# Splitting the expert weights in 24 pieces over the block loop instead of one expert an iteration

## The chip, the cores and the metric

One NeuronCore of one Trainium2 chip runs the whole kernel. The metric is the device time of one execution in microseconds. Five engines work side by side and meet only at semaphores: TensorE (PE; its weight loads are shown as PEld), VectorE (DVE), ScalarE (ACT), GpSimd (POOL), and SyncE (SP), which here only issues DMAs. ACT issues DMAs too.

## What is computed

64 images of 224 x 224 are embedded as 197 tokens of 192 features each (12,608 tokens); local attention (12 heads, 6 neighbours to each side) and a mixture of experts (2 of 8) follow, both with a residual:

```python
h = tok(x)                                   # patches @ W + b, class token, + pos_embed
h = h + local_attn(layernorm(h))             # window of +-6 tokens, 12 heads of 16
xn = layernorm(h)
top_w, top_i = top_k(softmax(xn @ router_w.T), 2);  top_w /= top_w.sum()
for e in range(8):
    w_e = sum(top_w * (top_i == e))
    out += w_e * (gelu(xn @ w1[e] + b1[e]) @ w2[e] + b2[e])      # 192 -> 768 -> 192
h = h + out
```

The products run in 16 bits with each 32-bit operand split in two halves: hi = f16(64 w), lo = f16(64 w - hi). For the expert weights the kernel makes those halves itself, from the f32 weights in HBM.

## The kernel before

There are two parts, one after the other. `attention_part` (some 935 us) embeds, attends, routes, and scatters the routed rows to a scratch in HBM, sorted by expert. `experts_part` (the rest) runs 73 batches of 384 sorted rows through the experts, with the split weights `w1s`, `w2s` that the first part leaves in SBUF.

`attention_part` goes over 53 blocks of 240 tokens. Every engine runs its own unrolled loop `pipeline(eng, body)` over iterations t = 0 to 61, and in iteration t each stage of the work has a block of its own: embedding, statistics and first normalisation have block t, the qk and v products t - 1, the scores t - 3, softmax and the product with v t - 4, projection and second normalisation t - 5, the router product t - 6. So from t = 53 on there is nothing to embed. Routing proper (choosing two experts, counting places) runs for two blocks at once: its part 0 on DVE in odd iterations, its parts 1, 2 and 3 in even ones. Between part 1 and part 2 TensorE counts with matmuls over `marks` (L794). Each engine's order within an iteration is that of its `body`:

- TensorE: counts (even t), turn of `xs`, of `os`, of `prob` (L812), of `payload`, qk product (L832), router (L844), v (L851), projection (L863), product with v (L877), scores (L885, L893), and then the 24 f32 matmuls of the next embedding (L775, 4.1 us).
- DVE: second normalisation, routing part 1, sum of the embedding (L644), statistics, part 2, first normalisation (L568), part 3, part 0 (begins at L594), low half of qk (L670), residual `h2` (L683), statistics, `on` (L694), the **expert split** (L700, L702), row maximum (L708), shift (L713).
- ACT: issue of the **expert's load** (L454, L455), issue of four `k_diag` copies (L461), exp (L465), `payload` (L471), `xT` (L481), `oT`, `xT2`, `pT`, `logit` (L505), qk high half (L511), v, `xs` (L522), issue of the `h2` output (L528), the **expert's high halves** (L536, L537), `os` (L542).
- POOL: low halves (L401, L413, L423), the reciprocal roots (L381, L384), and the scatter of the routed rows by indirect DMA (L391), four an iteration.

An expert's weights come as two loads, `stage1` [128, 3, 768] (1152 KB) and `stage2` [128, 6, 192] (576 KB), into one buffer each. `expert_loaded(t)` gives expert t - 1 for t = 1 to 7, and expert 7 for t = 53. In that iteration ACT issues both loads at the top (after DVE is through with the expert before) and multiplies near its end; DVE subtracts before it takes up the scores:

```python
act.wait_ge(s["staged"], 32 * (e + 1))
act.mul(w1s[0][:, e], stage1[:], WS)
act.mul(w2s[0][:, e], stage2[:], WS).then_inc(s["split_hi"], 1)
```

SP waits in iteration 56 until all experts are split, since the tables at the end of the part lie in `stage1`.

Of the kernel before, what the change touches and what calls it, by code (L numbers as in the profile page):

```python
# [21 lines left out]
ALU = mybir.AluOpType  # L22
# [88 lines left out]

EARLY = 7


def expert_loaded(t):


    if 1 <= t <= EARLY:  # L120
        return t - 1
    if BLOCKS <= t < BLOCKS + EXPERTS - EARLY:
        return t - BLOCKS + EARLY
    return None


def vit_tower(nc, xt, w_embed, bias_tab, pos, w_qk, w_v, w_p, b_p, router, w1, b1, w2, b2,
# [19 lines left out]
def attention_part(nc, xt, w_embed, bias_tab, pos, w_qk, w_v, w_p, b_p, router, w1, w2, b1, ident, band,  # L147
# [6 lines left out]
    with ExitStack() as ctx:  # L154
# [124 lines left out]
        def _(sp):  # L279
# [28 lines left out]
            def body(t):  # L308
                g, a = t - 2, t - 4
                if runs(t, 4):  # L310

                    sp.wait_ge(s["qk_lo_set"], min(a + 2, BLOCKS))
                    need(sp, s["scored"], 2 * a)
                    for h in range(8):
                        sp.dma_start(*key_halves(h, a)).then_inc(s["k_diag_set"], 16)
                if runs(t, 3):
                    load_band(t - 3)

                if runs(t, 0) and t > 0:
                    need(sp, s["embedded"], t - 1)  # L320
                    sp.dma_start(patches[t % 2][:], xt[t]).then_inc(s_patch[t % 2], 16)
                    need(sp, s["h1_set"], t - 1)
                    load_tab(t)
                if runs(t, 2):

                    sp.wait_ge(s["v_set"], g + 1)
                    sp.dma_start(v_dram[REACH + SPAN * g:REACH + SPAN * g + SPAN, :].rearrange("(n p) c -> p n c", n=2),
                                 v_rows[:].rearrange("p n h d -> p n (h d)")).then_inc(s["v_out"], 16)
                if runs(t, 4):

                    if a == 0:
                        sp.wait_ge(s["pad_set"], 32)
                    sp.wait_ge(s["v_out"], 16 * min(a + 2, BLOCKS))
                    need(sp, s["pv_done"], a)
                    for r in range(TRIO):
                        src = bass.AP(v_handle, SPAN * a * VCOLS + r * QUADS * (DH + 1),
                                      [[VCOLS, KEYS], [QUERIES * VCOLS, WINDOWS], [1, QUADS * (DH + 1)]])
                        cols = slice(r * QUADS * (DH + 1), (r + 1) * QUADS * (DH + 1))
                        sp.dma_start(v_diag[r * KEYS:(r + 1) * KEYS, :, cols], src).then_inc(s["v_in"], 16)
                if t == EARLY - 1:  # L340
                    sp.dma_start(b1s[:], b1).then_inc(s["later_in"], 16)
                if t == BLOCKS + 2:
                    sp.wait_ge(s["embedded"], BLOCKS)
                    sp.dma_start(fill_rows, fill).then_inc(s["later_in"], 16)
                if t == BLOCKS + 3:
                    sp.wait_ge(s["split_lo"], EXPERTS)
                    sp.dma_start(number, numbers).then_inc(s["later_in"], 16)
                    sp.dma_start(base, region_at[0:1, :]).then_inc(s["later_in"], 16)

# [82 lines left out]
        def _(act):  # L432
# [13 lines left out]

            def body(t):
                f, g, a, c, d, b = t, t - 1, t - 3, t - 4, t - 5, t - 6
                e = expert_loaded(t)
                if e is not None:  # L450
                    if e == 0:
                        act.wait_ge(s["setup2"], 2)
                    need(act, s["split_lo"], e)
                    act.dma_start(stage1[:], w1[e]).then_inc(s["staged"], 16)  # L454
                    act.dma_start(stage2[:], w2[e]).then_inc(s["staged"], 16)  # L455
                if runs(t, 3):
# [66 lines left out]
                if runs(t, 5):  # L523
# [5 lines left out]
                    else:  # L529
                        for n in range(2):  # L530
                            rows = tile_rows(d, n)
                            act.dma_start(out[at + ROWS * n:at + ROWS * n + rows, :], h2[0:rows, n, :]).then_inc(s["h2_out"], 16)
                if e is not None:

                    act.wait_ge(s["staged"], 32 * (e + 1))
                    act.mul(w1s[0][:, e], stage1[:], WS)  # L536
                    act.mul(w2s[0][:, e], stage2[:], WS).then_inc(s["split_hi"], 1)  # L537
                if runs(t, 4):

# [8 lines left out]
        def _(dve):  # L548
# [83 lines left out]
            def body(t):  # L632
# [28 lines left out]
                                             op0=ALU.mult, op1=ALU.subtract).then_inc(s["setup2"], 1)  # L661
                if due:
                    route_steps(grp, 3)
                if due_0:
                    route_steps(grp_0, 0)
                if runs(t, 1):
# [20 lines left out]
                if runs(t, 4):  # L687
# [5 lines left out]
                    need(dve, s["o_lo_set"], c)  # L693
                    dve.tensor_tensor(on[:].rearrange("p n (h e) -> p n h e", h=HEADS), o[:, :, :, 0:DH],  # L694
                                      rden[:].unsqueeze(3).to_broadcast([128, 2, HEADS, DH]), ALU.mult).then_inc(s["norm_done"], 1)
                e = expert_loaded(t)
                if e is not None:

                    dve.wait_ge(s["split_hi"], e + 1)
                    dve.scalar_tensor_tensor(out=w1s[1][:, e], in0=stage1[:, 0:2, :], scalar=WS, in1=w1s[0][:, e, 0:2, :],  # L700
                                             op0=ALU.mult, op1=ALU.subtract)
                    dve.scalar_tensor_tensor(out=w2s[1][:, e], in0=stage2[:], scalar=WS, in1=w2s[0][:, e],  # L702
                                             op0=ALU.mult, op1=ALU.subtract).then_inc(s["split_lo"], 1)
                if runs(t, 3):

                    for n in range(2):
# [481 lines left out]
```

## Time and profile before

| | us |
|---|---|
| median of 3 runs | 1693.18 |
| lowest, highest | 1689.94, 1693.35 |
| the profiled execution | 1697.55 |
| its span | 1695.8 |
| its attention part, about | 935 |

| engine | busy us | share of the span |
|---|---|---|
| TensorE (PE) | 1491.4 | 88% |
| DVE | 1121.2 | 66% |
| POOL | 861.2 | 51% |
| ACT | 718.4 | 42% |

The profile is of one execution. A slice of the page's time lines is 1/40 of the span, 42.4 us; a digit is a share in tenths. In what follows "interval t" is the time from the start of L644 (DVE's sum for block t) to the same instruction for block t + 1: it comes once an iteration and marks the beat of the pipeline.

### The profile page before, as it was taken

The numbers are of one execution on the slowest core, as the hardware profiler recorded it, in microseconds if no ns is written. First come the engines' busy times: TensorE is split into PE (matmuls) and PEld (weight loads), VectorE is DVE, ScalarE is ACT, GpSimd is POOL, SyncE is SP. The second block draws the span as 40 slices with busy tenths as digits, with TensorE's granted clock in tenths as the row PEclk, the third lists the DMA queues.
The fourth block names the chain that finished last, engine by engine and source line by source line (L and its number), as shares of the span: only waits on it lengthen the run. The fifth ranks groups of instructions, "written<-read, shape, count | busy, mean of one in ns | idle before, by whom it ended". The sixth has DMA issues, their size and how long they took to land. (4 is left out here: it accounts for less than half of the span.)

```text
span 1695.8 us, 52298 instructions
## 1 busy us (share of the span) xinstructions
PE 1491.4 (88%) x18345; PEld 1238.1 (73%) x18346; DVE 1121.2 (66%) x2875; ACT 718.4 (42%) x1201; POOL 861.2 (51%) x900
## 2 busy tenths in 40 slices
PE   4777999999999999899562799999999999999995
PEld 4666888888888788788451577777777777777774
DVE  3466777778777776777645466666666666666663
ACT  2443444444444444444421444444444444444441
POOL 3122656656555555555535155545554555455544
PEclk9887999999999999999865799999999999999998
DMA  6654555555555555555422334443444334433432
GB/s 206 205 172 126 157 148 154 153 151 155 144 150 154 150 152 145 143 139 150 113 76 95 93 59 60 60 65 57 59 60 65 57 59 60 65 58 59 59 45 29
DMA packets 190164, 182.64 MB, mean 108 GB/s; under 512 B 86361, under 2 KB 166437, under 8 KB 188989
## 3 DMA queue, kind: packets, MB, share of 16 engines
q1 hardware_dynamic: 125834, 111.46, 23.7%
q0 software_dynamic: 41680, 41.84, 16.8%
q10 hardware_dynamic: 22499, 27.28, 4.9%
q8 instruction: 101, 1.65, 0.4%
q14 instruction: 50, 0.41, 0.1%
HBM read 104.93 MB, written 65.29 MB: 100 GB/s over the span
## 5 line engine op out<-in xcount | busy, mean ns | idle before, releaser
L988 POOL DMA_INDIRECT out<-y,token x219 | 368.5, 1683 | 73.7 <-issue 72.9
L1096 PE MATMUL down<-w_hi,g_hi 128*128 x1314 | 323.7, 246 | 1.9 <-DVE y L1062 1.1
L1098 PE MATMUL down<-w_hi,g_lo 128*128 x1314 | 323.0, 246 | 0.0
L1097 PE MATMUL down<-w_lo,g_hi 128*128 x1314 | 322.9, 246 | 0.0
L1084 PE MATMUL up<-e_xT,w_hi 128*128 128x384 f16 x1314 | 286.7, 327 | 0.0
L1009 ACT ACTIVATE act_out<-up,bias 128x384 f32<-128x384 f32 x438 | 250.9, 581 | 73.3 <-PE up L1084 73.2
L391 POOL DMA_INDIRECT sorted_scratch<-payload,place x212 | 219.5, 1035 | 59.9 <-issue 56.9
L775 PE MATMUL near<-we,patches 128*120 128x192 f32 x1272 | 226.2, 335 | 17.4 <-DMA patches<-in_xt 10.0
L1001 ACT COPY e_xT<-turned 128x1152 f16<-128x1152 f16 x73 | 81.6, 1118 | 353.8 <-PE turned L1076 353.8
L775 PEld LDWEIGHTS near<-we,patches 128*120 128x120 f32 x1272 | 210.2, 187 | 27.8 <-issue 27.7
L1045 DVE TENSOR_TENSOR g_lo<-act_out,g_hi 128x768 f16<-128x768 f32 x219 | 209.9, 958 | 7.6
L1084 PE MATMUL up<-e_xT,w_lo 128*128 128x384 f16 x876 | 214.8, 327 | 0.0
L1043 DVE CAST g_hi<-act_out 128x768 f16<-128x768 f32 x219 | 123.1, 562 | 96.8 <-ACT act_out L1009 87.7
L1084 PEld LDWEIGHTS up<-e_xT,w_hi 128*128 x1314 | 126.0, 98 | 76.4 <-issue 1.2
L986 POOL TENSOR_TENSOR e_carrier<-e_carrier 32x1 f32<-32x1 f32 x73 | 13.3, 183 | 292.8 <-DVE y L1064 285.1
L1096 PEld LDWEIGHTS down<-w_hi,g_hi 128*128 128x128 f16 x1314 | 127.6, 97 | 29.0 <-issue 25.2
L1062 DVE TENSOR_TENSOR y<-down,bias 128x576 f32<-128x576 f32 x73 | 55.3, 758 | 133.2 <-PE down L1098 133.2
L1097 PEld LDWEIGHTS down<-w_lo,g_hi 128*128 128x128 f16 x1314 | 127.6, 97 | 1.3
L1098 PEld LDWEIGHTS down<-w_hi,g_lo 128*128 128x128 f16 x1314 | 128.3, 98 | 0.0
L1084 PEld LDWEIGHTS up<-e_xT,w_lo 128*128 x876 | 86.0, 98 | 57.3 <-issue 1.0
L465 ACT ACTIVATE prob<-prob 128x1008 f32<-128x1008 f32 x53 | 55.3, 1043 | 158.9 <-issue 89.1
L413 POOL TENSOR_TENSOR xs<-xn,xs 120x384 f16<-120x384 f32 x53 | 49.8, 939 | 141.3 <-ACT xs L522 141.3
(154 smaller groups left out, 2745.9 us busy)
## 6 DMA issues: line engine op xcount, KB each, us to landing
patches<-in_xt SPq DMA_DIRECT2D x53, 720.0 KB
rows<-sorted_scratch SPq DMA_DIRECT2D x73, 301.5 KB, 2.8
v_diag<-v_scratch SPq DMA_DIRECT2D x159, 89.2 KB
v_scratch<-v_rows SPq DMA_DIRECT2D x53, 191.2 KB, 3.0
tab<-tab_scratch SPq DMA_DIRECT2D x53, 180.0 KB
out<-h ACTq DMA_DIRECT2D x52, 180.0 KB
stage<-in_w ACTq DMA_DIRECT2D x8, 1152.0 KB
k_diag<-qk SPq DMA_DIRECT2D x424, 15.8 KB
```

What stands on the lines that cost most here:

```text
L391: pool.indirect_dma_start(out=sorted_dram, out_offset=bass.IndirectOffsetOnAxis(ap=at, axis=0), in_=payload[0:rows, 2 * (block % RING) + n ...
L465: act.activation(flat, flat, ACT.Exp, scale=DH ** -0.5 / (WS * WS)).then_inc(s["exp_set"], 1)
L775: ins = pe.matmul(near[0:ROWS, n * D:n * D + D], patches[f % 2][:, x, n * ROWS:n * ROWS + ROWS], we[:, x, :], start=(x == 0), stop=(x == K ...
L988: pool.indirect_dma_start(out=out, out_offset=bass.IndirectOffsetOnAxis(ap=token[k][:, n:n + 1], axis=0), in_=y[k % 2][:, n, :], in_offset ...
L1001: act.copy(xT[k % 2][:].rearrange("p n c r -> p (n c r)"), turned[:].rearrange("p b n -> p (b n)").bitcast(F16)[:, 0:3 * BATCH])\
L1009: act.activation(act_out[:, m, :], up[m % 3][:], ACT.Gelu, bias=bias[k % 2][:, m:m + 1], scale=1.0 / WS)\
L1043: dve.tensor_copy(g_hi[k % 2][:, m, :], act_out[:, m, :]).then_inc(s["hi_done"], 1)
L1045: dve.tensor_tensor(g_lo[k % 2][:, m, :], act_out[:, m, :], g_hi[k % 2][:, m, :], ALU.subtract).then_inc(s["lo_done"], 1)
L1084: ins = pe.matmul(up[m % 3][:], w1s[h][:, bass.ds(e, 1), w, 128 * m:128 * m + 128].rearrange("p a c -> p (a c)"), xT[k % 2][:, :, c, :], s ...
L1096: pe.matmul(dst, g_hi[k % 2][:, m, cols], high, start=(m == 0), stop=False)
L1097: pe.matmul(dst, g_hi[k % 2][:, m, cols], low, start=False, stop=False)
L1098: ins = pe.matmul(dst, g_lo[k % 2][:, m, cols], high, start=False, stop=(m == MF - 1))
```

## The change

An expert is split in three pieces: piece 0 is the first 768 columns of `w1`, piece 1 the rest of `w1` (for the high half two groups of 768, for the low half one), piece 2 is `w2`. The 24 pieces are given to DVE in iterations 4, 5, 6 and then in the odd ones from 9 to 49. ACT multiplies a piece one iteration ahead of DVE (t = 3, 4, 5, 8, 10, ..., 48) and issues an expert's loads at the top of the iteration of its piece 0: t = 3, 8, 14, 20, 26, 32, 38, 44. On DVE the piece stands behind the first normalisation and, in odd iterations, ahead of routing part 0; before it stood between `on` and the row maximum. SP's wait for the split weights moves from t = 56 to t = 51.

```diff
-EARLY = 7
-def expert_loaded(t):
-    if 1 <= t <= EARLY:
-        return t - 1
-    if BLOCKS <= t < BLOCKS + EXPERTS - EARLY:
-        return t - BLOCKS + EARLY
-    return None
+PIECES = 3
+PIECE_AT = [4, 5, 6, *range(9, BLOCKS, 2)][:PIECES * EXPERTS]
+assert len(PIECE_AT) == PIECES * EXPERTS
+def expert_piece(t):
+    n = PIECE_AT.index(t) if t in PIECE_AT else None
+    return (None, None) if n is None else divmod(n, PIECES)
...
-                if t == BLOCKS + 3:
-                    sp.wait_ge(s["split_lo"], EXPERTS)
+                if t == BLOCKS - 2:
+                    sp.wait_ge(s["split_lo"], PIECES * EXPERTS)
                     sp.dma_start(number, numbers).then_inc(s["later_in"], 16)
                     sp.dma_start(base, region_at[0:1, :]).then_inc(s["later_in"], 16)
...
-                e = expert_loaded(t)
-                if e is not None:
+                e, piece = expert_piece(t + 1)
+                if piece == 0:
                     if e == 0:
                         act.wait_ge(s["setup2"], 2)
-                    need(act, s["split_lo"], e)
+                    need(act, s["split_lo"], PIECES * e)
                     act.dma_start(stage1[:], w1[e]).then_inc(s["staged"], 16)
                     act.dma_start(stage2[:], w2[e]).then_inc(s["staged"], 16)
...
-                if e is not None:
+                if piece == 0:
                     act.wait_ge(s["staged"], 32 * (e + 1))
-                    act.mul(w1s[0][:, e], stage1[:], WS)
+                    act.mul(w1s[0][:, e, 0, :], stage1[:, 0, :], WS).then_inc(s["split_hi"], 1)
+                if piece == 1:
+                    act.mul(w1s[0][:, e, 1:3, :], stage1[:, 1:3, :], WS).then_inc(s["split_hi"], 1)
+                if piece == 2:
                     act.mul(w2s[0][:, e], stage2[:], WS).then_inc(s["split_hi"], 1)
...
                 if due:
                     route_steps(grp, 3)
+                e, piece = expert_piece(t)
+                if e is not None:
+                    dve.wait_ge(s["split_hi"], PIECES * e + piece + 1)
+                    if piece == 2:
+                        ins = dve.scalar_tensor_tensor(out=w2s[1][:, e], in0=stage2[:], scalar=WS, in1=w2s[0][:, e], op0=ALU.mult, op1=ALU.subtract)
+                    else:
+                        ins = dve.scalar_tensor_tensor(out=w1s[1][:, e, piece, :], in0=stage1[:, piece, :], scalar=WS, in1=w1s[0][:, e, piece, :],
+                                                       op0=ALU.mult, op1=ALU.subtract)
+                    ins.then_inc(s["split_lo"], 1)
                 if due_0:
                     route_steps(grp_0, 0)
...
-                e = expert_loaded(t)
-                if e is not None:
-                    dve.wait_ge(s["split_hi"], e + 1)
-                    dve.scalar_tensor_tensor(out=w1s[1][:, e], in0=stage1[:, 0:2, :], scalar=WS, in1=w1s[0][:, e, 0:2, :],
-                                             op0=ALU.mult, op1=ALU.subtract)
-                    dve.scalar_tensor_tensor(out=w2s[1][:, e], in0=stage2[:], scalar=WS, in1=w2s[0][:, e],
-                                             op0=ALU.mult, op1=ALU.subtract).then_inc(s["split_lo"], 1)
```

## Rows read from the trace of the kernel before

**Rows 1.** The page, part 2: busy tenths of TensorE and its granted clock, 40 slices.
```profile
PE   4777999999999999899562799999999999999995
PEclk9887999999999999999865799999999999999998
```
**Rows 2.** Stretches cut at L644: length, busy us of each engine, granted clock, DMA share, GB/s.
```profile
30.11:40.76 10.65, 7.05 (x61) 6.59 (x58) 6.12 (x12) 5.48 (x6) 1.80 (x3) 1.00 0.42 109
40.76:53.60 12.84, 8.11 (x55) 7.21 (x55) 6.14 (x13) 5.58 (x6) 1.80 (x3) 0.87 0.47 163
53.60:72.31 18.71, 12.42 (x103) 10.39 (x104) 8.60 (x18) 5.54 (x6) 1.79 (x3) 0.73 0.63 194
72.31:171.31 99.00, 73.95 (x1023) 64.26 (x1021) 60.82 (x144) 44.26 (x64) 25.98 (x33) 0.83 0.51 160
130.55:154.18 23.63, 14.59 (x199) 12.58 (x199) 15.18 (x39) 11.35 (x17) 6.50 (x8) 0.79 0.55 178
185.58:199.77 14.19, 13.82 (x229) 12.49 (x230) 11.46 (x40) 6.45 (x14) 7.95 (x11) 1.00 0.55 150
432.55:447.55 15.00, 13.12 (x211) 11.36 (x208) 10.61 (x36) 6.85 (x14) 9.43 (x12) 1.00 0.58 155
549.68:565.53 15.85, 13.02 (x211) 11.23 (x208) 11.37 (x35) 7.66 (x15) 10.27 (x13) 1.00 0.57 152
565.53:580.95 15.42, 15.29 (x229) 13.64 (x230) 11.53 (x39) 6.24 (x11) 6.80 (x10) 0.89 0.48 136
```
**Rows 3.** Timeline, iteration 6: start, us, engine, line, operation, [idle before <-releaser].
```profile
107.57 0.53 ACTq L455 DMA_DIRECT2D stage<-in_w  x1
...
121.52 0.56 DVE L694 TENSOR_TENSOR on<-mixed,rden 128x384 f32<-128x384 f32 x1
122.77 1.15 ACT L537 ACTIVATE w_hi<-stage 128x1152 f16<-128x1152 f32 x1
123.95 1.76 DVE L700 SCALAR_TENSOR_TENSOR w_lo<-stage,w_hi 128x1536 f16<-128x1536 f32 x1 [1.87 <-ACT w_hi L537]
125.62 2.07 DVE L702 SCALAR_TENSOR_TENSOR w_lo<-stage,w_hi 128x1152 f16<-128x1152 f32 x1
127.61 1.26 DVE L708 TENSOR_REDUCE mx<-scores 128x12 f32<-128x504 f32 x2
```
**Rows 4.** Waits from 27 to 172 us: total us, times, longest.
```profile
PE scores L812 <- ACT prob L465: 17.9, 4, 5.4
```
**Rows 5.** Timeline, iteration 3: the first scores.
```profile
64.54 0.60 PE L885 MATMUL scores<-band,identb 128*128 128x504 bf16 x2 [1.83 <-DMA k_diag<-qk]
```
**Rows 6.** Timeline around iteration 53, the tail of the block loop.
```profile
819.18 1.25 ACTq L455 DMA_DIRECT2D stage<-in_w  x1
...
825.13 1.97 PE L812 MATMUL scores<-identf,prob 128*126 128x128 f32 x8 [4.25 <-ACT prob L465]
...
840.49 1.93 POOL L391 DMA_INDIRECT sorted_scratch<-payload,place  x1 [0.22 <-issue]
841.41 1.26 DVE L708 TENSOR_REDUCE mx<-scores 128x12 f32<-128x504 f32 x2
...
846.62 0.26 PE L794 MATMUL mixed<-marks,above 120*120 120x8 f16 x1 [10.82 <-DVE marks L605]
```
**Rows 7.** Timeline of the setup: a split of 768 columns on DVE.
```profile
20.47 0.95 DVE L657 SCALAR_TENSOR_TENSOR wqk_lo<-stage,wqk_hi 128x768 f16<-128x768 f32 x1
```
**Rows 8.** Timeline, iteration 27, odd and in steady state.
```profile
435.43 1.10 POOL L391 DMA_INDIRECT sorted_scratch<-payload,place  x1 [0.23 <-issue]
...
438.49 0.19 DVE L594 TENSOR_REDUCE top<-logit 120x4 f32<-120x32 f32 x1 [2.59 <-ACT logit L505]
...
439.98 0.92 POOL L413 TENSOR_TENSOR xs<-xn,xs 120x384 f16<-120x384 f32 x1 [2.15 <-ACT xs L522]
```
**Rows 9.** Waits from 172 to 808 us, the steady state.
```profile
ACT os L542 <- DVE on L694: 143.7, 43, 3.4
DVE top L594 <- ACT logit L505: 48.8, 22, 2.6
```

More of the change, by code:

```diff
@@ L339, in body @@
                         sp.dma_start(v_diag[r * KEYS:(r + 1) * KEYS, :, cols], src).then_inc(s["v_in"], 16)
-                if t == EARLY - 1:
+                if t == 6:
                     sp.dma_start(b1s[:], b1).then_inc(s["later_in"], 16)
```

## The prediction

> **What bounds the kernel now.** I read the page's time lines first [rows 1]. TensorE is near full through the expert part and the middle of the attention part. It is at 4 to 7 tenths in the first four slices and at 2 to 7 around the change of parts, and its granted clock is low in the same places. The expert part has no line in the diff, so all that can move lies in the first 935 us.
>
> Then I cut the attention part at DVE's L644, once an iteration [rows 2]. In steady state an even interval takes 14.19 us with TensorE busy for 13.82 at full clock: TensorE is the bound. An odd one takes 15.00 us with TensorE busy for 13.12, so something else holds it a little. Intervals 4 to 8 together take 99.0 us, 19.8 each, for no more work; interval 7 alone takes 23.63. Iterations 1 to 7 are those with an expert in them. TensorE idles there and then runs part of the time at half clock (a mean of 0.83 is a mix of its two levels, 2.4 and 1.2 GHz). Interval 8 has no expert, but it pays for what 7 left late.
>
> What holds them is seen in iteration 6 [rows 3]. DVE ends `on` at 122.08 (121.52 + 0.56). The scores are there, but it first waits 1.87 us for ACT's second multiplication, then subtracts for 1.76 and 2.07 us, and reaches the row maximum L708 at 127.61: **5.53 us late**. The embedding, 4.1 us, should cover shift and exp; it can't cover these 5.53 too, and TensorE waits for exp in four early iterations, 17.9 us in all, up to 5.4 at a time [rows 4].
>
> **The change part by part, against the profiled execution (1697.55 us; its span is 1695.8).** The shown median, 1693.18, is 4.4 us lower; I carry the difference over to it.
>
> *Intervals 4 to 8 without an expert ahead of L708.* They take 99.0 us. A floor is TensorE's busy time brought to full clock, busy x clock: 73.95 x 0.83 = 61.4 [rows 2]. For the estimate I take five steady intervals, 5 x (14.19 + 15.00) / 2 = 73.0, and leave out the work that these five don't have yet, since the pipeline is still filling: steady busy time is 5 x (13.82 + 13.12) / 2 = 67.4, so 67.4 - 61.4 = 6.0. That makes 67.0 and a gain of **32.0**. Its bounds: 37.6 by the floor, and 20.8 if all five run like the slowest steady pair, 15.85 and 15.42 [rows 2], with nothing left out (78.2).
>
> *Intervals 1 to 3.* Full clock busy time is 7.05, 8.11 x 0.87 = 7.1 and 12.42 x 0.73 = 9.1 [rows 2]. In 1 and 2, with the split gone from between qk and the next L644, I allow 0.5 us of latency on it: 7.6 each, for 10.65 and 12.84; 8.3 go. Interval 3 now has the first load at its top, and there TensorE stood for `k_diag` until 64.54 [rows 5], 10.9 us into the interval, since ACT's four copies queue behind 1.7 MB. They will again, so I let only 2.4 of its 18.71 go. Gain **10.7** (6 to 18; the high end is all three at their busy time).
>
> *The tail.* Iteration 53 pays the same gap with the same terms, 5.53 us up to L708 at 841.41, and TensorE stands 10.82 us before the counts that need the marks DVE makes after it [rows 6]. No embedding runs there to cover it, so all of it goes. The load's issue goes from ACT too: the second of the two took 1.25 us, and behind it TensorE waited 4.25 us for exp [rows 6]; I take 1.65 for both issues (0 to 2.7). Gain **7.2** (5.5 to 8.2). Past the marks every step hangs on the one before, so the gain reaches the change of parts.
>
> *DVE's 24 pieces.* A piece of w1 is 768 columns, 0.95 us [rows 7]. One of w2 is 1152 columns: 2.07 us in iteration 6, and halfway between 768 columns (0.95) and 1536 (1.76 [rows 3]) it would be 1.36; I take 1.36 and keep 2.07 for the range. The three early ones fall where DVE idles. Of the 21 others 14 cost 0.95 and 7 cost 1.36: 22.8 us. They stand in the wait of L594 for the logits, 2.59 us in iteration 27 [rows 8], 48.8 us over 22 odd iterations, a mean of 2.2 [rows 9]. The logits don't depend on the piece, so this wait is cover. It is not the same everywhere, and where it is under 1.36 a w2 piece sticks out by some tenths. Cost **1** (0 to 10: 21 pieces late by 0.5, for the rest of a scatter). Without the cover it would be the 22.8.
>
> *ACT's multiplications.* 1152 columns take 1.15 us [rows 3], so the largest piece, 1536, takes some 1.5. They stand in ACT's wait for `on`, 143.7 us over 43 iterations, a mean of 3.3 [rows 9]. Cost 0, and no gain: ACT is no bound. Where a load has not landed, ACT would wait with `os`, and so TensorE's turn of it, behind it. The multiplication comes near the end of the iteration whose top has the issue, and 1.7 MB in an early interval left no wait for a load among the longer ones; 0 too, and what it would be is in rival 1.
>
> *The eight loads.* They move from an early, half-empty pipeline into a full one, at the top of t = 8, 14, ..., 44 (seven; the one at t = 3 is above). ACT issues them ahead of `k_diag` and exp. The second load's issue took 0.53 us in iteration 6 [rows 3] and 1.25 in iteration 53 [rows 6]; with the first one, 0.9 to 1.6 before exp. In even iterations the counts stand on TensorE ahead of the turn that needs exp, which gives some cover. I take 0.5 each, **3.5** in all (0 to 11, by the full 1.6). The data itself, 1.7 MB beside 150 GB/s, fits an interval with a DMA share of 0.55 [rows 2].
>
> *SP's wait* at t = 51 is for pieces that DVE ended in iteration 49; SP has passed waits on later blocks by then. 0.
>
> Sum: 32.0 + 10.7 + 7.2 - 1 - 3.5 = **45.4 us**. The profiled execution would come to 1697.55 - 45.4 = 1652.2, the median to 1693.2 - 45.4 = 1647.8; I say 1648.
>
> **A row and a rule.** In iteration 53 a scatter on POOL took 1.93 us [rows 6] beside DVE's second subtraction, for 1.10 in iteration 27 [rows 8]: the two hinder each other. The Trainium skill, page "SBUF — State Buffer", section "Who interferes with whom", says that a DVE instruction with two SBUF inputs contends with a GpSimd instruction that reads SBUF, and the later one blocks until the other is through. By that rule a piece could also wait for a scatter that began before it, and the sum would be some 8 us less; where only the scatter waits, as in the row, it stays. No row here shows a subtraction that waits for a scatter. The third rival works the mechanism out from rows.
>
> **The rivals.**
>
> *1. The load hurts the full pipeline.* ACT's `k_diag` copies stand behind 1.7 MB in its queue. In interval 3 they landed 10.9 us after its start [rows 5], and a steady interval has only 14.19 for all. If they, or the load itself, come 1.5 us late, and the half clock follows (15.42 against 14.19, 1.2 us [rows 2]), seven loads cost 7 x 2.7 = 19 in place of 3.5: 1648 + 15.5 = 1663. For it: the scatters, which the early intervals didn't have. Against it: the scores come at the end of an interval. Chance 0.17.
>
> *2. The early intervals are bound by something else behind the split*, such as `k_diag` and patches through SP, and give back only half: 1648 + 21 = 1669. For it: a DMA share of 0.63 in interval 3 [rows 2]. Against it: TensorE's long wait there is for ACT's exp [rows 4]. Chance 0.08.
>
> *3. Slower: DVE becomes the bound of odd iterations.* From L594 to the marks DVE runs without a gap and is the longest chain of an odd interval. POOL's scatter (1.10 us at 435.43 [rows 8], another behind it) runs just where the piece starts. If the piece waits for both, 2.2 us from 435.9 where it would start, it ends at 439.0 or 439.5 and pushes L594 from 438.49 by 0.5 to 1.0. Later marks then collide with POOL's `payload` (interval 15.85 for 15.00, and 15.42 for 14.19 behind it [rows 2]: 2.1 us); six of 22 odd intervals are such now. With all 22: 21 x 0.7 + 16 x 2.1 = 48, and the loads at their worst, 11, make 59 against the 50 gained: 1693 + 9 = 1702. It decides from (50 - 3.5) / 21 = 2.2 us an odd iteration. Against it: POOL has 2.15 us to spare before L413 [rows 8] and half of DVE's wait is free. Chance 0.03. Its mild form, without the collisions, costs 8 and is in the range.
>
> *4. More than forecast:* intervals 4 to 8 at the floor, 3 near it, and later exps (by the load's issue) avoid some of the six collisions: 1648 - 15 = 1633. Chance 0.12.
>
> **How the numbers follow.** Forecast 0.60 (1637 to 1659 of its own), the rivals as given. The range, 1635 to 1668, holds the forecast, rival 1 and the near half of rival 4, 0.8 together; its ends also hold the pieces' 10 us or the loads' 11. A change within 0.2% (3.4 us) is about what a measurement can't tell from none. Faster by more has all but rival 3 and a little for a fault in the early sum: 0.95; same 0.02; slower 0.03.
>
> **What would show it.** Right: L694 followed at once by L708 in iterations 4 to 7 and 53; L644 for block 9 at about 129 instead of 171.3; clock near 1 from 65 us on; odd intervals at 15 or less; the counts after iteration 53 some 7 us nearer to it. The wait for the logits shrinks from 2.6 to about 1.6, with L594 no later in its interval. Wrong: a TensorE wait for `k_diag` in t = 8, 14, ..., 44; L594 without a wait before it; even intervals with a load at 16 us; intervals 4 to 8 at 16 or more.

## The result

The changed kernel takes 1641.42 us (median of 4 runs, 1638.75 to 1648.06), beside 1691.56 for the kernel before (1689.84 to 1693.35): a ratio of 0.9709, 95% interval 0.9675 to 0.9743, or 50 us less. The forecast was 1648, 45.4 us less. A second comparison on another chip gave 1632.40 beside 1685.36, a ratio of 0.9701 (0.9667 to 0.9735).

Line numbers shift a little in the changed kernel: L644 is L646 (`h`), L694 is L706 (`on`), L708 is L712 (row maximum), L594 is L596 (the wait for the logits), L605 is L607 (marks), L812 is L816, L885 is L889. DVE's pieces are L673 (w1, 768 columns) and L671 (w2, 1152 columns).

The profile after, its page's time lines (busy tenths and granted clock in 40 slices), which answer [rows 1]:

```profile
PE   5999999998989999998643999999999999999995
PEclk9999999999999999999656999999999999999998
```

TensorE is near full from the second slice on and its clock no longer falls in the first four. The dip at the change of parts stays.

The stretches of the kernel after, cut at L646 as [rows 2] at L644 (length, busy us of PE, PEld, DVE, ACT, POOL, granted clock, DMA share, GB/s): intervals 1 to 3, then 4 to 8, then 9 to 51; and single ones: 3, 7, an even one without a load (22), 35 and 36.

```profile
29.90:59.24 29.34, 24.09 (x219) 21.23 (x217) 12.14 (x33) 9.01 (x14) 5.41 (x9) 0.94 0.58 167
59.24:122.45 63.21, 61.68 (x1023) 55.02 (x1021) 49.01 (x138) 34.07 (x57) 21.53 (x33) 1.00 0.60 170
122.45:756.68 634.23, 580.94 (x9367) 513.06 (x9364) 498.37 (x1590) 316.24 (x559) 375.68 (x474) 0.99 0.60 167
...
45.16:59.24 14.08, 10.54 (x109) 8.27 (x107) 5.75 (x14) 4.19 (x6) 1.80 (x3) 0.88 0.69 203
95.17:108.48 13.31, 12.61 (x211) 11.22 (x208) 10.75 (x35) 6.17 (x12) 4.51 (x7) 1.00 0.66 192
313.34:327.58 14.24, 13.82 (x229) 12.48 (x230) 11.47 (x39) 8.40 (x15) 7.90 (x11) 1.00 0.53 149
505.15:520.99 15.84, 13.02 (x211) 11.22 (x208) 12.25 (x36) 7.67 (x15) 10.30 (x13) 1.00 0.57 152
520.99:536.40 15.41, 15.28 (x229) 13.86 (x230) 11.52 (x39) 6.89 (x12) 6.83 (x10) 0.89 0.49 135
```

The kernel before has for intervals 9 to 51:

```profile
171.31:808.02 636.71, 583.93 (x9367) 516.07 (x9363) 478.94 (x1569) 292.40 (x538) 373.87 (x474) 0.99 0.55 150
```

So intervals 4 to 8 went from 99.00 to 63.21 and 1 to 3 from 42.20 to 29.34. The 43 intervals behind them took in DVE's 21 pieces (19.4 us more of busy DVE) and ACT's multiplications and got no longer. The fourth stretch is the tail, from L646 of block 52 to the last turn of counts. Here are the counts of iteration 53 and the last ones on TensorE, after:

```profile
786.04 0.26 PE L798 MATMUL mixed<-marks,above 120*120 120x8 f16 x1 [4.51 <-issue]
...
856.52 0.26 PE L798 MATMUL mixed<-marks,above 120*120 120x8 f16 x1 [3.39 <-DVE marks L607]
```

Before, the last ones stood here, with L644 of block 52 at 808.02:

```profile
914.50 0.26 PE L794 MATMUL mixed<-marks,above 120*120 120x8 f16 x1 [3.42 <-issue]
```

That is 914.50 - 808.02 = 106.5 us before, and 856.52 - 756.68 = 99.8 after (6.6 less before rounding).

| step | before | after | gain | forecast |
|---|---|---|---|---|
| intervals 1 to 3 | 42.2 | 29.3 | 12.9 | 10.7 |
| intervals 4 to 8 | 99.0 | 63.2 | 35.8 | 32.0 |
| intervals 9 to 51 | 636.7 | 634.2 | 2.5 | -4.5 |
| tail | 106.5 | 99.8 | 6.6 | 7.2 |
| the rest of the span | | | 1.0 | 0 |
| span | 1695.8 | 1637.0 | 58.8 | 45.4 |

These are two single executions. That of before, 1697.55, lies 6 us over its median, that of after, 1638.75, 2.7 under its own; of the 58.8 the medians confirm 50. The sum of the prediction was made for the profiled execution: 1652.2, and 1638.75 was measured, 13.4 less. That the medians lie nearer (1648 and 1641.42) is in part luck, since the execution that was profiled before was one of the slower ones.

### The profile page after: what moved, and what is told of

It is laid out like the page before. It is cut to its first block and busy times, and to the rows that moved or that the text cites. A ratio compares the mean times of both kernels' runs of the same rounds, so it can differ in the third digit from the quotient of the medians.

```text
span 1637.0 us, 52314 instructions
## 1 busy us (share of the span) xinstructions
PE 1471.8 (90%) x18345; PEld 1222.1 (75%) x18346; DVE 1114.5 (68%) x2883; ACT 721.7 (44%) x1209; POOL 856.6 (52%) x900
## 5 line engine op out<-in xcount | busy, mean ns | idle before, releaser
L570 DVE TENSOR_SCALAR xn<-h,mv,rs 120x192 f32<-120x192 f32 x212 | 72.6, 384 | 65.3 <-POOL rs L383 65.3
```

The source lines that it names most:

```text
L570: ins = dve.tensor_scalar(xn[:, n, :], h[:, n, :], mv[:, n, 0:1], rs[:, n:n + 1], ALU.subtract, ALU.mult)
```

## The experiments

In what follows "the old place" is DVE's, between `on` and the row maximum, and a *collision* is this, seen in both kernels: POOL's `payload` subtraction starts while DVE does the last small steps up to the marks. Interval 35 of the kernel after has one:

```profile
519.88 0.19 DVE L590 TENSOR_TENSOR chosen<-tmp,best 120x32 f32<-120x32 f32 x1
520.11 0.96 DVE L607 TENSOR_TENSOR marks<-chosen 120x32 f16<-120x32 f32 x1
520.12 0.89 POOL L400 TENSOR_TENSOR payload<-xn,payload 120x384 f16<-120x384 f32 x1
521.12 0.22 PE L798 MATMUL mixed<-marks,above 120*120 120x8 f16 x1 [1.79 <-DVE marks L607]
```

The marks take 0.96 where they take 0.19 elsewhere, TensorE stands 1.79 us for them, and the next interval often runs at a clock of 0.89 and lasts 15.4. I count as one an odd interval with a small step of over 0.5 us in its last 3.2 us. Intervals 9 to 51 of the profiled executions; chips A, B and C differ (an even interval without a load takes 14.2 us on A, 14.1 on C and 13.77 on B), so between chips only ratios to the kernel before compare. The chip of the first two rows is not on record. Most of the difference between 14.2 and 13.77 lies in one wait. In interval 22 the router's products end 4.98 us after the start, in the kernel after and in no_loads alike. ACT's copy of `logit` begins at 5.01 in no_loads (chip B) and at 5.80 in the kernel after, and only there does TensorE wait for it, 0.28 us. What holds ACT is open.

| kernel | chip | ratio to before | intervals 9 to 51 | collisions, of 22 | even intervals at a clock under 0.95 |
|---|---|---|---|---|---|
| before | | 1 | 636.7 | 6 | 5 |
| after | | 0.9709 | 634.2 | 4 | 3 |
| old_place | A | 0.9977 | 691.6 | 11 | 20 |
| twice | A | 0.9725 | 643.5 | 6 | 7 |
| whole | A | 0.9912 | 665.0 | 7 | 8 |
| tail_part | A | 1.0001 | 633.2 | 5 | 4 |
| no_loads | B | 0.9663 | 603.7 | 6 | 2 |
| marks_first | B | 0.9605 | 599.6 | 0 | 0 |
| old_place_marks | B | 0.9844 | 638.2 | 0 | 14 |
| before_marks | B | 0.9892 | 594.3 | 0 | 0 |
| after again | C | 0.9701 | 629.2 | 4 | 1 |
| loads_moved | C | 0.9662 | 630.8 | 4 | 3 |
| best | C | 0.9618 | 620.8 | 0 | 1 |

### old_place: the pieces, but where the split stood before

```diff
@@ DVE, block loop
                 if due:
                     route_steps(grp, 3)
-                (the piece: wait for split_hi, one subtraction)
                 if due_0:
                     route_steps(grp_0, 0)
...
                                       rden[:].unsqueeze(3).to_broadcast([128, 2, HEADS, DH]), ALU.mult).then_inc(s["norm_done"], 1)
+                (the piece)
```

> The changed kernel with one thing undone: DVE's 24 pieces stand again between `on` and the row maximum; their number, their iterations, ACT's part and the loads stay as changed. Theory P (the place counts: from the logits to the marks DVE is the longest chain of an odd iteration, while ahead of the logits it waits): 14 x 0.95 + 7 x 1.35 = 22.8 us of pieces go into the chain, and later marks meet POOL's payload more often, up to 2.1 us each; 1641 + 23 to 1641 + 45, so 1664 to 1686 us. Theory S (the size counts: pieces of about 1 us are covered by the embedding's 4.1 us wherever they stand): within 5 us of the changed kernel's 1641.

Measured: 1687.56 (1679.39 to 1695.53), ratio 0.9977 (0.9953 to 1.0002). Its intervals 1 to 3 and 4 to 8 take 29.2 and 62.6, as in the kernel after; all 57 us are lost from interval 9 on. Spreading the pieces over the iterations therefore gives the early gain wherever on DVE they stand, and the place decides whether it is kept. An odd interval and the even one behind it, first DVE's and ACT's timeline, then the two stretches:

```profile
546.24 0.56 DVE L696 TENSOR_TENSOR on<-mixed,rden 128x384 f32<-128x384 f32 x1
546.72 0.95 DVE L705 SCALAR_TENSOR_TENSOR w_lo<-stage,w_hi 128x768 f16<-128x768 f32 x1
547.58 1.27 DVE L712 TENSOR_REDUCE mx<-scores 128x12 f32<-128x504 f32 x2
550.06 1.04 ACT L464 ACTIVATE prob<-prob 128x1008 f32<-128x1008 f32 x1 [2.71 <-DVE prob L717]
...
551.64 0.89 DVE L590 TENSOR_TENSOR chosen<-tmp,best 120x32 f32<-120x32 f32 x1
```
```profile
536.09:552.66 16.57, 12.95 (x211) 11.20 (x208) 12.17 (x36) 7.17 (x14) 10.09 (x13) 0.99 0.55 146
552.66:569.40 16.74, 16.60 (x229) 15.07 (x230) 11.66 (x39) 6.72 (x12) 6.78 (x9) 0.81 0.43 119
```

The row maximum comes 0.95 us late and all behind it, the marks too. 28 us are in the odd intervals, 29 in the even ones, where TensorE's clock has fallen: 20 of 21 run under 0.95, at a mean of 16.1 us. The cost is 57 / 21 = 2.7 us a piece of 0.95 to 1.35 in the traces, 46 / 21 = 2.2 in the medians; 1687.56 is just above the 1686 that theory P had as its top.

### twice: DVE does each subtraction twice, at the new place

```diff
                     dve.wait_ge(s["split_hi"], PIECES * e + piece + 1)
                     if piece == 2:
+                        dve.scalar_tensor_tensor(out=w2s[1][:, e], ...).then_inc(s["once"], 1)
+                        dve.wait_ge(s["once"], PIECES * e + piece + 1)
                         ins = dve.scalar_tensor_tensor(out=w2s[1][:, e], ...
                     else:
+                        (the same two lines for w1s)
```

> The changed kernel with every subtraction on DVE done twice, one right behind the other, at the new place: 22.8 us more of DVE's work. If DVE's wait for the logits is the cover (in the changed kernel 23.5 us of it are left over in 19 odd iterations, 1.2 each), a second 0.95 fits and a second 1.35 sticks out by some tenths to 1 us: 1641 + 2 to 1641 + 9, and the wait for the logits falls to a few us in all. If instead DVE's busy time counts as such: 1641 + 23 = 1664 or more.

Measured: 1646.06 (1643.29 to 1647.86), ratio 0.9725 (0.9697 to 0.9752): by the medians 4.6 us more than the kernel after, for 22.8 us more of DVE. The intervals of the two ratios overlap (0.9675 to 0.9743 for the kernel after); at their far ends they are 13 us apart, still well under 22.8. DVE's wait for the logits falls to 6.3 us in 8 iterations. It covers a second subtraction almost as well as the first, so the first can't have cost more than a little.

### whole: whole experts at the new place

```diff
-PIECE_AT = [4, 5, 6, *range(9, BLOCKS, 2)][:PIECES * EXPERTS]
+EXPERT_AT = [*range(5, 5 + 2 * EXPERTS, 2)]
...
                if e is not None:
+                    for piece in range(PIECES):
                         dve.wait_ge(s["split_hi"], PIECES * e + piece + 1)
```

> The changed kernel with whole experts at the new place: all three pieces of an expert in one iteration, t = 5, 7, ..., 19, ACT one iteration ahead. 3.25 us of DVE's work stand in a wait of 1.8 to 2.6 us. By the theory that the place counts only what sticks out is paid: about 1 us in each of the six full iterations and up to 2.1 more where the marks come too late; the loads come every second iteration. 1641 + 5 to 1641 + 20, so 1646 to 1661. By the theory that an expert in one go costs what it cost before (5.5 us and the half clock): 8 x 5.5 = 44, so 1685.

Measured: 1678.88 (1672.92 to 1679.45), ratio 0.9912 (0.9881 to 0.9943): a miss, 18 us over the top. An iteration with an expert (13), ACT, then DVE with one row of POOL:

```profile
192.53 0.84 ACT L533 ACTIVATE w_hi<-stage 128x768 f16<-128x768 f32 x1 [1.94 <-DVE h L692]
193.28 1.47 ACT L534 ACTIVATE w_hi<-stage 128x1536 f16<-128x1536 f32 x1
194.66 1.15 ACT L535 ACTIVATE w_hi<-stage 128x1152 f16<-128x1152 f32 x1
195.71 0.50 ACT L540 CAST os<-on 128x384 f16<-128x384 f32 x1
...
201.78 0.67 DVE L566 TENSOR_SCALAR xn<-h,mv,rs 120x192 f32<-120x192 f32 x2 [2.63 <-POOL rs L381]
202.36 1.82 DVE L670 SCALAR_TENSOR_TENSOR w_lo<-stage,w_hi 128x768 f16<-128x768 f32 x2
203.39 2.93 POOL L388 DMA_INDIRECT sorted_scratch<-payload,place  x1 [0.30 <-issue]
204.10 1.35 DVE L668 SCALAR_TENSOR_TENSOR w_lo<-stage,w_hi 128x1152 f16<-128x1152 f32 x1
205.37 0.18 DVE L592 TENSOR_REDUCE top<-logit 120x4 f32<-120x32 f32 x1
205.81 1.51 DVE L594 SCALAR_TENSOR_TENSOR tmp<-logit,rank 120x32 f32<-120x32 f32 x1
```

Three engines run late at once. ACT multiplies for 3.3 us, and its copy of `os` follows with no wait before it: in the kernel after it waits up to 3.5 us there. DVE's three subtractions fill 3.1 us and L592 follows with no wait either. And POOL's second scatter, which begins while DVE subtracts, takes 2.93 us for 1.00, in each of the six iterations with an expert from 9 on; L594 then takes 1.51 us for 0.19 beside the end of that scatter and POOL's next subtraction. That interval takes 17.89 us. So at the new place the size of a step decides: one piece fits the cover, three don't. The expectation had priced DVE's part alone. Beside the kernel after, intervals 4 to 8, in which no scatter meets a piece, lose 12.1 us (75.35 for 63.21) and 9 to 51 lose 30.8; no run tells the shares of the three engines apart.

### tail_part: of the change only the last expert

```diff
-    if BLOCKS <= t < BLOCKS + EXPERTS - EARLY:
-        return t - BLOCKS + EARLY
+LAST_AT = [45, 47, 49]
...
+                piece = last_piece(t)
+                if piece is not None:
+                    (DVE's piece of expert 7, at the new place)
```

> The kernel before with one part of the change: expert 7 alone goes out of iteration 53 and comes in three pieces at t = 45, 47, 49 behind the first normalisation, its load at t = 44; experts 0 to 6 stay one an iteration at t = 1 to 7. By the prediction's terms: the tail's 7.2 us gained, 0.5 for the load and about 0.2 for the pieces lost: 1691.6 - 6.5 = 1685 us. If the gain of the tail were given back later (the tail bound by something else), 1691.

Measured: 1692.22 (1680.92 to 1697.99), ratio 1.0001 (0.9975 to 1.0028). Its trace has the gain: L644's counterpart for block 52 at 802.70, the counts of iteration 53 and the last ones at

```profile
832.47 0.26 PE L824 MATMUL mixed<-marks,above 120*120 120x8 f16 x1 [4.51 <-issue]
...
902.56 0.26 PE L824 MATMUL mixed<-marks,above 120*120 120x8 f16 x1 [3.42 <-issue]
```

that is 99.9 us where before took 106.5. What follows the last counts takes 781.8 us there and 781.3 before, so the trace doesn't give the gain back. The medians don't show it: 1692.22 beside 1691.76, for the 1685 that was expected, and the interval of the ratio allows a gain of 4 us at most. The single runs spread over 17 us, and the kernel before's over 12 in the same comparison. So the gain of the tail is seen in two traces and is not confirmed by the times; what offsets it in the other executions is open.

### no_loads: one load for all experts

```diff
-                if piece == 0:
+                if piece == 0 and e == 0:
...
-                    act.wait_ge(s["staged"], 32 * (e + 1))
+                    act.wait_ge(s["staged"], 32)
```

> The changed kernel with the load of the first expert alone: all 24 pieces are made from its weights, so experts 1 to 7 get wrong weights and the output differs; all else is done as before. It takes away the seven loads at t = 8, 14, ..., 44. Forecast of the prediction: they cost 3.5, so 1638. Rival 1 of the prediction (the load delays k_diag and halves the clock): 19, so 1622. From the trace, the seven intervals are 0 to 1.4 longer than their neighbours, 4.1 in all: 1637.

Measured: 1606.28 (1604.42 to 1613.08) beside 1664.67 for before on that chip, ratio 0.9663 (0.9611 to 0.9716). From 0.9709 and 0.9701 that is 6 to 8 us less, with an interval of about 8 on it. In the trace six of the seven even intervals take 13.77 us, like all others. The forecast of 3.5 fits, and so would twice that; rival 1's 19 doesn't. Another measure on the same chip is marks_first, below, which has the loads: its seven intervals with a load take 5.8 us more than 7 x 13.77.

### marks_first, old_place_marks, before_marks: no collisions

The same three lines in the kernel after, in old_place and in the kernel before:

```diff
@@ POOL, block loop
                 if runs(t, 6):
 
+                    grp, due = groups(t, 8)
+                    if due:
+                        pool.wait_ge(s["marks_set"], grp + 1)
                     pool.wait_ge(s["hi2"], b + 1)
```

> The changed kernel, with one wait more on POOL: in the iterations with marks it starts the payload subtraction only when DVE has set the marks, so that the two no longer run at the same time. Theory C (collisions cost time): three odd intervals of the changed kernel's trace last 15.5 us or more (15, 35, 45) with an even one of 15.4 at a clock of 0.89 behind them; without them 3 x 1.5 go, and no interval from 9 on is over 15.3. 1636 to 1640, and a narrower spread of single runs. Theory N (the overlap is a mark of a late interval, not its cause): 1641 within 2, the long intervals stay. It could cost instead, if payload then comes late for the transposes on TensorE: 1645 or more.

Measured: 1599.66 (1594.31 to 1600.55), ratio 0.9605 (0.9556 to 0.9654). No_loads ran on the same chip and shows the price of one collision. Interval 35, no_loads with a mark of 0.96, then marks_first with one of 0.19:

```profile
486.74:501.01 14.27, 12.78 (x211) 11.17 (x208) 12.39 (x36) 7.26 (x15) 10.14 (x13) 1.00 0.61 164
```
```profile
487.48:500.98 13.50, 12.78 (x211) 11.14 (x208) 11.61 (x37) 7.26 (x15) 9.28 (x12) 1.00 0.62 168
```

0.77 us of interval for 0.77 us of marks, with the same busy TensorE and ACT (POOL's 0.86 more is the `payload` that starts ahead of the cut). `payload` pays little: POOL waited 11 times for the marks, 3.6 us in all, and TensorE's wait for `payload` is 4.9 us for 4.0 in no_loads (120 to 735 us), while its wait for the marks is 16.8 for 22.2. So a collision costs about its own length, and that the two run at the same time is its cause: theory C's mechanism.

Its size and one of its signs were not met. On chip A's scale 0.9605 is 1625 us, below theory C's 1636 to 1640; and intervals 20 and 44, both with a load, take 15.75 and 15.33. The kernel after was not run on chip B, so the gain of 16 to 17 us rests on ratios from different chips, each with an interval of 6 to 8 us. An estimate on chip B alone: no_loads' 1606.28 and 3.9 to 5.8 for the loads make 1610 to 1612 for the kernel after, so the wait gives 10 to 12.

> The changed kernel with DVE's piece back between on and the row maximum (1687.6 us), and with POOL's wait for the marks. It parts the 46 us that the old place costs. If they are mainly collisions and the half clock behind them (16 or so odd intervals more than in the changed kernel, at 1.5 to 2.1 each), about 25 to 33 go and it comes to 1655 to 1663. If it is the piece itself on the chain from on to exp (1.1 us in 21 iterations and TensorE stopped for it), hardly anything goes: 1680 to 1688.

Measured: 1637.59 (1636.29 to 1639.57), ratio 0.9844 (0.9796 to 0.9891). On chip A's scale that is 1665, between what the two theories had. 0.0133 of the ratio, 22 us, goes by the three lines. That is near the 25 to 33 of the first theory, and yet it doesn't bear it out, for the kernel after loses 0.0104 by the same lines. Without collisions the old place still costs 1637.59 - 1599.66 = 38 us on the same chip, a ratio of 0.024, where it cost 0.027 with them. So it is mainly the second theory: the row maximum comes late and TensorE stands for it, and what that theory had left out, the half clock behind many of the stops: 14 of 21 even intervals still take 15.4 us at a clock of 0.89.

> The kernel before with POOL's wait for the marks alone. Its trace has six odd intervals of over 15.5 us, each followed by one at a lower clock, 2.1 us a pair: theory C expects 1679 to 1684, and a narrower spread of single runs than the 12 us that the kernel before has shown; theory N 1691.6 within 2.

Measured: 1647.16 (1642.67 to 1648.39), ratio 0.9892 (0.9842 to 0.9941), 17.5 us less: faster than either theory had it. The trace has no mark over 0.19 and no odd interval over 15.5. The same three lines gave 7 us on chip C (best against loads_moved) and, by the ratios, 16 to 17 on B (marks_first against 0.9701 and 0.9709). That they help is shown on two chips, before_marks and best beside kernels of their own chip; how much is not settled, and the six visible pairs of the kernel before, 2.1 us each, make only 13 of the 17.5.

### The kernel after again, loads_moved and best

> The changed kernel as it is, as the level for the two that follow: 0.971 of the kernel before, within 0.003 (0.9709 in its first comparison).

Measured: 1632.40 (1630.29 to 1637.7), ratio 0.9701.

```diff
-                if piece == 0:
-                    if e == 0:
-                        act.wait_ge(s["setup2"], 2)
+                if t == 1:
+                    act.wait_ge(s["setup2"], 2)
+                    act.dma_start(stage1[:], w1[0]).then_inc(s["staged"], 16)
+                    act.dma_start(stage2[:], w2[0]).then_inc(s["staged"], 16)
...
@@ ACT, behind the h2 output of iteration t
+                e2, piece2 = expert_piece(t + 2)
+                if piece2 == 0 and e2 > 0:
+                    need(act, s["split_lo"], PIECES * e2)
+                    (the two loads of expert e2)
```

> The changed kernel with its loads issued elsewhere on ACT: the first at the top of iteration 1 in place of 3, and the seven others behind the h2 output of the odd iteration before, where ACT has waited some 3 us for on, in place of ahead of k_diag and exp. Theory L (the issue ahead of k_diag and exp, and the copies behind 1.7 MB, cost the seven intervals 0.5 to 1.5 each, and interval 3 its wait for k_diag of 2.69 and the half clock behind it): 3.5 to 7 less for the seven and 3 to 4 for the first, 7 to 10 in all, a ratio of 0.965 to 0.967. Theory N (nothing is bound there): 0.971. If a load then holds up k_diag or v_diag of the odd iteration instead, 0.972 or more.

Measured: 1627.74 (1624.38 to 1635.08), ratio 0.9662 (0.9629 to 0.9694): 0.0039 and by the medians 4.7 us under the kernel after on the same chip. The ratio is where theory L had it, the microseconds are below its 7 to 10, and the interval of the ratio overlaps that of the kernel after (0.9667 to 0.9735), so the gain is likely and not shown. What the issue does is seen in iteration 44 of the kernel after, on ACT:

```profile
633.12 0.51 ACT L544 CAST os<-on 128x384 f16<-128x384 f32 x1 [3.39 <-DVE on L706]
633.13 0.68 ACTq L453 DMA_DIRECT2D stage<-in_w  x1
633.85 0.68 ACTq L454 DMA_DIRECT2D stage<-in_w  x1
634.62 3.31 ACTq L460 DMA_DIRECT2D k_diag<-qk  x4
637.97 1.04 ACT L464 ACTIVATE prob<-prob 128x1008 f32<-128x1008 f32 x1 [4.33 <-issue]
```

The two load issues take 1.36 us and stand, with the four for `k_diag`, ahead of the exp, for which the shifted scores were ready at 635.45: the exp starts 2.5 us after them, and the interval takes 15.55 us. The four `k_diag` issues are not longer for the load: in iterations without one they take 2.44 to 3.81 us in the same trace. What differs is the load's own issue. In the two traces of the kernel after, the five intervals in which it took 1.35 to 1.9 us last 15.0 to 15.6 us, and the nine in which it took 0.8 to 1.0 last 14.0 to 14.7.

In loads_moved interval 44 takes 14.20 us, for 15.04 in the kernel after on that chip, but interval 20 takes 16.57 for 14.68, so part of the gain is lost again. TensorE stops there between the 24 products of the first half of the scores and the 24 of the second, where the program has no wait:

```profile
291.61 0.83 PE L900 MATMUL scores<-k_diag,qk 128*32 128x336 f16 x24
294.53 0.83 PE L900 MATMUL scores<-k_diag,qk 128*32 128x336 f16 x24 [2.10 <-issue]
```

Such stops of 0.57 to 2.10 us stand in intervals 8, 20 and 32 of loads_moved, best and marks_first, six in all and each in an interval with a load; in the kernel after the longest is 0.32 (interval 32 of its second profile). So a load seems to hurt in a second way as well; what holds TensorE there is open.

The first load brought nothing. Interval 3 of the kernel after, then of best, which has the same early load (TensorE's timeline):

```profile
51.52 1.02 PE L889 MATMUL scores<-band,identb 128*128 128x504 bf16 x2 [2.69 <-DMA k_diag<-qk]
```
```profile
49.59 0.60 PE L895 MATMUL scores<-band,identb 128*128 128x504 bf16 x2 [0.67 <-DMA k_diag<-qk]
54.06 5.84 PE L785 MATMUL near<-we,patches 128*120 128x192 f32 x24 [2.46 <-DMA patches<-in_xt]
```

The wait for `k_diag` falls from 2.69 to 0.67, and a wait of 2.46 for the patches takes its place; the interval lasts 14.68 us for 14.08 (14.09 in the kernel after on the same chip). SP issues the patches behind its eight `k_diag` copies (5.4 us of issuing there).

> loads_moved with POOL's wait for the marks as well. In the runs with that wait alone the ratio to the kernel before was 0.9605 for 0.971 of the changed kernel. If both gains are there and add: 0.954 to 0.957. If the loads' part lies in the same wait that the marks take away: 0.960.

Measured: 1620.87 (1616.27 to 1621.76), ratio 0.9618 (0.9586 to 0.9650): 11.5 us under the kernel after on the same chip. It beats both kernels. It is short of the 0.954 to 0.957 of two full gains and near the 0.960 of one; with an interval of 0.003 it can't be told whether it is better than marks_first alone (0.9605 on another chip).

## Why the prediction was right, point by point

**Intervals 4 to 8: right, a little small.** The step from `on` to the row maximum is 90.09 + 0.56 to 90.57 in iteration 6 now, no gap, for 5.53 us in [rows 3]:

```profile
84.77 0.67 DVE L570 TENSOR_SCALAR xn<-h,mv,rs 120x192 f32<-120x192 f32 x2 [1.08 <-POOL rs L383]
85.36 1.35 DVE L671 SCALAR_TENSOR_TENSOR w_lo<-stage,w_hi 128x1152 f16<-128x1152 f32 x1
...
90.09 0.56 DVE L706 TENSOR_TENSOR on<-mixed,rden 128x384 f32<-128x384 f32 x1
90.57 1.26 DVE L712 TENSOR_REDUCE mx<-scores 128x12 f32<-128x504 f32 x2
```

L646 for block 9 stands at 122.45, forecast about 129: 3.8 of the difference are these intervals, 2.2 the three before. The five intervals take 63.21 at full clock, 1.8 over the floor of 61.4 worked out before. The 67.0 carried the steady pipeline's own idle time (73.0 against 67.4) into intervals that have no marks before the end of the seventh (first at 108.38) and no scatter before the end of the eighth (first at 120.44); that this is why they were too high is argued, not tested. The floor was the better estimate.

**Intervals 1 to 3: right.** 7.63 and 7.63 as forecast; interval 3 took 14.08 for 16.3. The wait for `k_diag` stayed, 2.69 us in place of 1.83 [rows 5], but the first load, named as its cause, was half the story: with it out of the way the patches end last (rival 2 had named them).

**The tail: right in the traces.** 6.6 for 7.2, though the times of tail_part don't confirm it. The gap is gone at the counts of iteration 53 (29.4 us after L646 of block 52 for 38.6 in [rows 6], 9.2 earlier) and 2.6 of it is given back by the last counts.

**DVE's pieces: right, and the chief risk was rightly placed.** All 24 take one of two durations, in the view by tile:

```profile
L673 DVE SCALAR_TENSOR_TENSOR w_lo<-stage,w_hi x16: 951/952/955, 62.5 to 687.3; 128x768 f16<-128x768 f32 x16
L671 DVE SCALAR_TENSOR_TENSOR w_lo<-stage,w_hi x8: 1351/1352/1354, 85.4 to 717.8; 128x1152 f16<-128x1152 f32 x8
```

The interpolated 1.36 was right: a subtraction of w2 took 1.35 in the kernel before too where it was alone, and 2.07 beside POOL's `os` (in iteration 53 `os` starts at 838.24 and takes 2.03 for 0.91). DVE's wait for the logits, 48.8 us in 22 [rows 9], is now

```profile
DVE top L596 <- ACT logit L504: 25.2, 20, 1.9
```

from 122 to 765 us: 23.6 us of the cover used for 22.8 of pieces, and in two of the 22 iterations none left. Twice shows that even then little is lost. That the place mattered was forecast as 22.8 us "without the cover"; old_place shows 46. The mis-sized part is what follows a late row maximum: the half clock in the even interval, 29 of the 57 us in the trace. Of the signs, "odd intervals at 15 or less" came only in part: their mean went from 15.07 to 14.88, and 14 of 22 last 15.01 to 15.84.

**The row and the rule.** The prediction read its row as the two hindering each other. Only the scatter was hindered: in iteration 6 the subtraction took the same 2.07 us with no scatter about. In the kernel after, a piece of w2 meets two scatters:

```profile
448.09 1.11 POOL L390 DMA_INDIRECT sorted_scratch<-payload,place  x1 [0.23 <-issue]
448.48 1.35 DVE L671 SCALAR_TENSOR_TENSOR w_lo<-stage,w_hi 128x1152 f16<-128x1152 f32 x1
449.50 1.20 POOL L390 DMA_INDIRECT sorted_scratch<-payload,place  x1 [0.30 <-issue]
```

The piece begins during the first and neither is lengthened, here and in all 21 such cases: 0.95 or 1.35 us for the piece, and 1.10 to 1.11 for the scatter, as in [rows 8], where no piece stands. The second scatter begins with 0.33 us of the piece left and takes 1.20 for 1.00, in all seven cases. With 1.00 left it took the 1.93 of [rows 6], and with 2.06 left of two subtractions in a row the 2.93 in whole. So it takes what is left of DVE's subtractions and 0.87 to 0.93 us more. In twice that is not so 14 times: a scatter that begins within 0.04 us of a subtraction of 768 columns keeps its 0.99 to 1.00, and the subtraction takes 1.02 to 1.03 for 0.95.

So the 8 us were not there, and rival 3's place was harmless. The Trainium skill, page "SBUF — State Buffer", section "Who interferes with whom", says that a two-input DVE instruction contends with a GpSimd instruction that reads SBUF, and that one holds the port for its whole length. For POOL's subtractions the traces agree that one waits for the other (marks 0.19 to 0.96 beside `payload`, though the record of the marks begins 0.01 us first). For a scatter they agree only where DVE was first.

**The loads: right in sum, at the low end.** The seven intervals are 14.0 to 15.6, together 3.9 over 7 x 14.19, for 3.5; the other measures are 5.8 on chip B and 6 to 8 by ratios. Rival 1's delay by `k_diag` doesn't show in the kernel after: TensorE doesn't stop at the scores of these intervals in its first profile, and for 0.32 us at most in its second. Where there was a loss, the load's issue ahead of exp was long.

**Intervals 9 to 51: the forecast cost of 4.5 was a gain of 2.5.** Part of that is collisions and the low-clock intervals behind them: 6 and 5 before, 4 and 3 after, and 4 and 1 in its second profile (629.2). At 0.9 and 1.1 us (15.6 against 14.7, 15.4 against 14.3) two fewer of each make 4 of the 7 us. Rival 4 named later exps as a way to it. Nothing in the runs shows that the change does this rather than chance: twice has 6 again with a slightly longer chain, and tail_part, with three pieces and one load in these intervals, takes 633.2 us, 3.5 less than the kernel before. That the pieces, the loads and the rest came out as a gain is therefore luck as far as the runs show. This is where single executions differ by ten us, and why the 58.8 of the two profiles are 50 in the medians.

## What to carry to other kernels

A step of work that must be done somewhere is nearly free where its engine waits for something that does not depend on it, up to the length of that wait, and cost about twice its own length (2.2 to 2.7 us for 1.1) where the next turn of the full engine hangs on it. Measure the cover by the wait in a steady iteration, on every engine that the step touches, and cut the step to fit. Then look for short steps that grow five-fold (0.19 to 0.96 us) when another engine's work falls on them: a wait that orders the two can gain more than it costs.

## What the runs showed of the hardware

- A DVE addition of 32 columns with two inputs from SBUF (the marks) took 0.96 us, for 0.19, when a POOL subtraction of 384 columns (0.89) began with it. A DVE subtraction of 768 or 1152 columns that began during a scatter on POOL was not lengthened (0.95 and 1.35 us, 21 times). A scatter that began during such a subtraction took what was left of it and 0.87 to 0.93 us more: 1.20 with 0.33 left, 1.93 with 1.00, 2.93 with 2.06, for 1.00 alone.
- A stop of TensorE of some 1.8 us before the counts is often followed by an even interval at a granted clock of 0.89, a mix of 2.4 and 1.2 GHz, that takes 15.4 us for 14.2: behind 5 of 6 such stops in the kernel before, 3 of 4 in the kernel after and 1 of 4 in its second profile. In old_place, behind stops of 2.0 to 3.0 us, nine even intervals ran at 0.80 to 0.81 and took 16.7 to 17.0, and others behind stops as long at 0.89 and 15.4.
- The four `k_diag` issues on ACT took 2.44 to 3.81 us in the kernel after, with a load before them or without; the two issues of a load took 0.8 to 1.9.
- The same program's even interval took 13.77 us on one chip and 14.1 and 14.2 on two others, at a granted clock of 1.00 on each; the kernel before took 1664.67 there, for 1685.36 and 1691.76.
